# Preparing the look-ups and corner weights of far samples eight rounds at once, ahead of their gathers

## The reference, cut to what matters

```python
loc_x = px + kx + off[..., 0];  loc_y = py + ky + off[..., 1]
x0 = floor(loc_x);  y0 = floor(loc_y);  wx = loc_x - x0;  wy = loc_y - y0
sampled = corner(y0, x0, (1-wy)*(1-wx)) + corner(y0, x0+1, (1-wy)*wx) \
        + corner(y0+1, x0, wy*(1-wx)) + corner(y0+1, x0+1, wy*wx)   # corners outside the image give 0
out = einsum('nhwkgc,nhwkg->nhwgc', sampled, mask) @ output_proj_w.T + output_proj_b
```

## Time and profile before

| | |
|---|---|
| median of 3 runs | 3149.86 us (3148.06 to 3168.16) |
| the profiled execution | 3152.57 us, span 3150.9 us |
| busy: PE, DVE, ACT, POOL | 86%, 85%, 57%, 40% of the span |
| value stage, first image | about 1597 to 1666 us |
| group stage, first image | about 1670 to 2346 us |
| value stage, second image | about 2407 to 2475 us |
| group stage, second image | about 2480 to 3144 us |
| far lists, rounds in them | 16, 52 in all: 3 3 3 3 5 3 2 4 and 3 3 3 4 3 4 3 3 |

### The profile page before, as it was taken

How to read it: one execution, slowest core, us unless ns; L and a number is a source line. 1 busy time by engine, 2 the same in 40 slices (tenths; PEclk the granted TensorE clock), 3 DMA queues, 4 the chain that set the end, 5 groups by cost and what they waited for, 6 DMA issues and landing times.

```text
span 3150.9 us, 78127 instructions
## 1 busy us (share of the span) xinstructions
PE 2720.6 (86%) x22424; PEld 2186.8 (69%) x22424; DVE 2677.2 (85%) x6553; ACT 1781.7 (57%) x3476; POOL 1273.8 (40%) x1837
## 2 busy tenths in 40 slices
PE   1888888999999999999676999989987879999999
PEld 0555555556555655656566888988876778889888
DVE  3788888888888888888666999989987779999998
ACT  0788888888888888888342333433212333344331
POOL 3333332323333333332435444653560554554541
PEclk9999999999999999999888999999999899999999
DMA  7898897889888888889664445444444544444443
GB/s 183 150 166 159 163 163 134 138 142 144 138 144 136 143 139 141 140 141 143 192 202 123 130 144 151 138 136 141 122 148 144 173 125 127 140 129 125 136 114 109
DMA packets 429629, 453.44 MB, mean 144 GB/s; under 512 B 80781, under 2 KB 346397, under 8 KB 428420
## 3 DMA queue, kind: packets, MB, share of 16 engines
q1 hardware_dynamic: 414276, 442.74, 63.7%
q0 software_dynamic: 15168, 8.36, 2.2%
HBM read 294.58 MB, written 156.62 MB: 143 GB/s over the span
## 4 chain that ended last, share of the span: by engine, by line
DVE 25%; issue 9%; DMA 7%; PE 5%; POOL 3%; DVEq 1%; POOLq 1%; ACT 1%; SPq 0%; ACTq 0%
DVE prod L1731 18%; DMA vring<-vals 3%; DVE tt L1715 2%; PE sum_ps L1529 1%; DMA vring<-attended 1%; DMA o_sel<-off_out,pos 1%; DVE my L1710 1%; DVE x L1742 1%; POOL gath L1311 1%; PE wt_ps L1459 1%; DVE x L1646 1%; PE om_ps L1444 1%; PE sum_ps L1481 1%; PE sum_ps L1430 1%; DVE reach L1667 1%
## 5 line engine op out<-in xcount | busy, mean ns | idle before, releaser
L753 ACT ACTIVATE prob<-sbias,nmax 128x256 f32<-128x256 f32 x2048 | 904.0, 501 | 203.0 <-DVE nmax L846 200.6
L846 DVE CUSTOM_DVE_ANT_0 sbias<-s_ps,nbias 128x256 f32<-128x256 f32 x2048 | 768.0, 420 | 212.3 <-PE s_ps L638 201.4
L1731 DVE TENSOR_TENSOR prod<-vring,wt_ps 128x1920 f32<-128x1920 f32 (+3 forms) x512 | 900.9, 1812 | 14.1 <-DMA vring<-vals 12.0
L1481 PE MATMUL sum_ps<-ident,prod 128*128 128x128 f32 x6400 | 751.2, 275 | 24.9 <-DVE prod L1731 24.5
L651 PE MATMUL pt_ps<-ident,prob 128*128 128x128 f32 x4096 | 644.3, 280 | 141.1 <-ACT prob L753 138.0
L1481 PEld LDWEIGHTS sum_ps<-ident,prod 128*128 128x128 f32 x6400 | 719.4, 142 | 66.3 <-DVE prod L1731 42.3
L651 PEld LDWEIGHTS pt_ps<-ident,prob 128*128 128x128 f32 x4096 | 447.3, 140 | 285.1 <-DVE probT L855 133.4
L1583 ACT ACTIVATE hat<-off,one_col 128x576 f32<-128x576 f32 x128 | 140.2, 1095 | 619.3 <-DVE tt L1715 619.3
L571 POOL CAST parts<-qk 128x1024 bf16<-128x1024 f32 x64 | 66.3, 1036 | 869.5 <-ACT qk L746 869.5
L638 PE MATMUL s_ps<-stack 96*128 96x256 bf16 x2048 | 396.1, 274 | 9.0 <-DMA stack<-parts_dram 7.8
L855 DVE COPY probT<-pt_ps 128x512 f32<-128x512 f32 x512 | 351.8, 687 | 12.0 <-PE pt_ps L651 12.0
(11 more groups left out here) (183 smaller groups left out, 3444.4 us busy)
## 6 DMA issues: line engine op xcount, KB each, us to landing
stack<-parts_dram SPq DMA_DIRECT2D x768, 128.0 KB, 7.6
vring<-vals SPq DMA_DIRECT2D x270, 320.0 KB, 3.0
parts_dram<-parts SPq DMA_DIRECT2D x64, 768.0 KB, 6.6
off_out<-off SPq DMA_DIRECT2D x64, 432.0 KB, 4.0
strips<-x SPq DMA_DIRECT2D x68, 256.0 KB, 3.7
far_sums<-nothing SPq DMA_DIRECT2D x64, 256.0 KB, 2.1
attended<-on SPq DMA_DIRECT2D x256, 64.0 KB
x<-x SPq DMA_DIRECT2D x64, 256.0 KB, 4.7
```

Of the source, the lines that this page charges most:

```text
L753: ins = nc.scalar.activation(prob[:, n % 4, half, :], sbias[:, n % SBIAS, half, :], ACT.Exp, bias=nmax[:, n % SBIAS, half:half + 1], scale ...
L846: ins = nc.vector.tensor_tensor_reduce(out=sbias[:, n % SBIAS, half, :], in0=s_ps[:, n % 2, half, :], in1=nbias[:, h, half, :], scale=1.0, ...
L1481: mm = nc.tensor.matmul(sum_ps[:, par, r * H:(r + 1) * H], prod[:, r % 2, dx, dy * C:(dy + 1) * C], ident[:], start=(r + dx + dy == 0), st ...
L1731: nc.vector.tensor_tensor(prod[:, r % 2, first:last].rearrange("p a (t c) -> p (a t) c", c=CG), vring[:, at:at + wide].rearrange("p a (t c ...
```

## The change

- **Rounds at once.** `prepare(e, slot)` issues the look-ups of all 8 possible rounds of an epoch (16 indirect DMAs, two semaphores in turn, so that pair t waits for pair t - 2), then `corner_weights` computes place, index and weights of all 8 rounds with wide small instructions. It waits only for `flags` and for the offsets in DRAM, not for the count of rounds. `far_list` then runs the rounds, each only with a copy of its index, two gathers, three arithmetic steps and the scatter. The gathers of round t + 1 are issued inside round t.
- **Order on POOL.** In each image `prepare` of epoch 0 stands before the wait for the stored `vals`; `prepare` of epoch e + 1 stands behind list e.
- **No mf.** `find_far` no longer computes `mf`; `tap_terms` reads the mask straight from `off`, every third number. The hat functions of a far sample are zero on all but the corners that fall on near taps, and the near taps keep these; `corner_weights` sets the same corners to zero in the far part (`edge`, `held`).
- **Value stage.** From v = 12 ACT normalises every step; POOL is done with v = 11. `flags` of epoch 0 moves from behind v = 7 to behind v = 10. PE makes both halves of group 0's weights after v = 24, and DVE's `tap_terms` of group 1 stands between the value stage and group 0 instead of inside group 0.

```diff
-                for v in (*range(1, V_LAST, 2), *range(V_LAST, GROUPS)):
+                for v in range(1, V_FIRST, 2):
                     normalise(v)
-                for slot in range(VROWS):
-                    pool.wait_ge(vrow_out[slot], count((b + 1) * (4 * GROUPS)))
...
+                def corner_weights(n, flagged):
+                    step(nc.gpsimd.tensor_tensor(wm[:, 0:n], o_sel[:, 0:n, 2], flagged, ALU.mult))
+                    step(nc.gpsimd.tensor_scalar(sidx[:, 0:n], i_sel[:, 0:n, 3], sum_e[:, 0:1], None, ALU.add))
...
+                    then(nc.gpsimd.tensor_tensor(w4[:, 0:n], w4[:, 0:n], held[:, 0:n], ALU.mult))
+
+                def gather_corners(index):
+                    then(nc.gpsimd.tensor_copy(idx1[:], index))
                     for dx in range(2):
-                        gather(gath[:, dx, :], table, idx[:], gathered, dx * YP * C)
...
+                        gather(gath[:, dx, :], table, idx1[:], gathered, dx * YP * C)
+                def far_round(weights, place, look_ahead):
                     pool.wait_ge(gathered, 32)
                     clear(gathered)
...
+                    look_ahead()
                     then(nc.gpsimd.tensor_tensor(gsum[:, 0], gsum[:, 0], gsum[:, 1], ALU.add))
+                    pool.wait_ge(scattered, 16)
+                    clear(scattered)
+                    step(nc.gpsimd.tensor_copy(sidx1[:], place))
                     then(nc.gpsimd.tensor_tensor(gval[:], gsum[:, 0, 0], gsum[:, 0, 1], ALU.add))
...
+                def prepare(e, slot):
+                    n = b * EPOCHS + e
+                    pool.wait_ge(key_ready, count(5 * n + 5))
+                    pool.wait_ge(off_stored, count(16 * (b * GROUPS + EPOCH * (e + 1) + RING_O)))
+                    epoch_base(e)
+                    for t in range(ROUNDS):
+                        if t >= 2:
+                            pool.wait_ge(fetched[t % 2], 32 * (t // 2))
+                        look_up(t, far_at[:, slot, 0, t:t + 1], far_at[:, slot, 1, t:t + 1])
+                    for par in range(2):
+                        pool.wait_ge(fetched[par], 32 * (ROUNDS // 2))
+                        clear(fetched[par])
+                    corner_weights(ROUNDS, far[:, slot, 0:ROUNDS])
...
+                prepare(0, 0)
+                for slot in range(VROWS):
+                    pool.wait_ge(vrow_out[slot], count((b + 1) * (4 * GROUPS)))
+                with pool.Fori(0, EPOCHS // RING_E - 1) as i:
                     for slot in range(RING_E):
+                        far_list(RING_E * i + slot, slot)
+                        prepare(RING_E * i + slot + 1, (slot + 1) % RING_E)
+                far_list(EPOCHS - RING_E, 0)
+                prepare(EPOCHS - 1, 1)
+                far_list(EPOCHS - 1, 1)
...
-                    nc.vector.scalar_tensor_tensor(out=mf[:, s.place], in0=reach[:], scalar=1.0,
-                                                   in1=off[:, s.place, :, :, 2],
-                                                   op0=ALU.is_le, op1=ALU.mult).then_inc(det_step, 1)
...
-                    nc.vector.tensor_tensor(my[:], hat[:, :, :, KG:], mf[:, s.place].unsqueeze(1)
+                    nc.vector.tensor_tensor(my[:], hat[:, :, :, KG:], off[:, s.place, :, :, 2].unsqueeze(1)
...
-                        if v == 2 * EPOCH - 1:
+                        if v == V_FIRST - 2:
                             flags(first_spot(EPOCH - 1))
...
                 each_step(dve, value)
+                tap_terms(first_spot(1))
                 each_group(dve, group)
```

More of the change, by code:

```diff
@@ L1044, in deformable @@
         gathered = ctx.enter_context(nc.semaphore("gathered"))
-        fetched = ctx.enter_context(nc.semaphore("fetched"))
+        fetched = [ctx.enter_context(nc.semaphore(f"fetched{par}")) for par in range(2)]
         scattered = ctx.enter_context(nc.semaphore("scattered"))
         off_stored = sem("off_stored")
+        no_index = sem("no_index")
         block = ctx.enter_context(nc.Block())
@@ L1319, in clear, with look_up @@
                     pool.sem_clear(s)
-                def look_up():
-                    gather(i_sel[:], info_out, pos[:, 0:1], fetched)
-                    gather(o_sel[:], off_now[0], pos[:, 1:2], fetched)
+                def look_up(t, info_at, off_at):
+                    gather(i_sel[:, t, :], info_out, info_at, fetched[t % 2])
+                    gather(o_sel[:, t, :], off_now[0], off_at, fetched[t % 2])
                 def epoch_base(e):
@@ new lines, in far_rest @@
+                                step(nc.gpsimd.tensor_copy(rest_at[:, 0:1], rest_atf[:]))
+                                then(nc.gpsimd.tensor_scalar(rest_at[:, 1:2], rest_atf[:], row_at[:, 0:1], None, ALU.add))
+                                look_up(0, rest_at[:, 0:1], rest_at[:, 1:2])
+                                pool.wait_ge(fetched[0], 32)
+                                clear(fetched[0])
+                                corner_weights(1, is_far[:])
+                                gather_corners(idx[:, 0:1])
@@ L1504, in group @@
                     par = s.place % 2
-                    weights(s.q, 1)
+                    if not isinstance(s.q, int) or s.q > 0:
+                        weights(s.q, 1)
                     taps(s.q, par, 0)
@@ L1537, in value @@
                         if v == V_LAST:
-                            weights(0, 0)
+                            for half in range(HALVES):
+                                weights(0, half)
                 each_step(pe, value)
@@ L1754, in group @@
                     products(s.q, par, 1)
-                    if s.has(1):
+                    if s.has(1) and (not isinstance(s.q, int) or s.q > 0):
                         tap_terms(s.on(1))
```

170 lines of the change are left out of this document (89 added, 81 removed).

## The result

| | before | changed |
|---|---|---|
| median | 3157.82 us (3148.06 to 3168.16, 4 runs) | 3239.38 us (3232.99 to 3243.93, 4 runs) |
| profiled execution, its span | 3152.57, 3150.9 | 3236.43, 3234.8 |
| busy: PE, DVE, ACT, POOL | 86%, 85%, 57%, 40% | 85%, 83%, 56%, 40% |

The change is slower: ratio 1.0247, 95% interval 1.022 to 1.0274, some 80 us. My range ended at 3137. The runs are compared as ratios to runs of the kernel before on the same chip, whose median lay between 3151 and 3164.

What follows compares the result with a forecast made beforehand. Three of 16 far lists, the first of each image and the fifth of the first, were taken to bound the kernel through their length. 32 + 7 + 3.4 = 42.4 us off 3152.57 gave 3110, as median 3108; range 3082 to 3137.

Steps and rivals of the forecast that it cites:

- the length of prepare: On POOL, look-ups and corner weights of all 8 rounds: 36 us, 41 for epoch 0; bounds 31 to 61.
- the later lists: POOL's prepare plus list, 67 us for 3 rounds or 74 for 4, fits the epoch of some 82 us: no cost.
- the epoch of 81.9 us: Sign in the changed profile: 81.9 us between two MAX8 of DVE, 82.7 before less mf.
- a new round: In POOL's list, scatter to scatter: 7.6 us where it took 13.14.
- both first lists in time: First list of each image ready about when PE asks for fsum: 16 us saved each, 32 in all; bounds 8 to 18 each.
- fifth list: List of 5 rounds in the first image done before it is needed: 7 us saved, bounds 0 to 7.
- mf and `my` together: On DVE, mf dropped saves 0.47 us a group, my's strided mask read adds 0.32: 3.4 us less in all.
- value stage: Value stage and group 0: DVE's course 1.4 us earlier in each image; bounds 3 later to 4 earlier.
- the first (lists stay late): Prepare of epoch 0 ends late, PE still waits 12 to 15 us at first lists: 3138 us, chance 0.19.
- the second (a stride that costs nothing): DVE's my reads the mask with its stride at no cost: 19 us more gained, 3089 us, chance 0.14.
- The third: POOL becomes the bound from a prepare of 52 us, every list late: near 3200 to about 3270 us, chance 0.09.
- The fourth: prepare(0) waits for something stored late and starts 5 us later; inside the forecast's range, no chance of its own.

Runs made afterwards that it cites:

- four rounds ahead: The changed kernel with rounds 0 to 3 looked up in prepare, rounds 4 to 7 inside the list only where it has more than 4 rounds: 3122.84 us, ratio 0.9879.
- late prepare: Prepare of epoch 0 put behind the wait for the stored vals: 3147.75 us against four rounds ahead as base, 3286.42 us on the changed kernel.
- four rounds alone: The changed kernel with look-ups for rounds 0 to 3 only, the fifth round of one list left out of the output: 3120.39 us, ratio 0.9875.
- paced run: The changed kernel with each pair of look-ups waiting for the pair just before it, not the one two back: 3171.18 us, ratio 1.004.
- burst on the old kernel: The kernel before with 16 more indirect look-ups, read by nobody, behind every list: 3275.71 us, ratio 1.0369.
- the one with indices of round 0: The changed kernel with all eight pairs of look-ups taking the indices of round 0: 3259.47 us, ratio 1.0315.
- six rounds ahead: The kernel with four rounds ahead, now with six, so 12 look-ups in a prepare: 3175.64 us, ratio 1.004.
- the break in the burst: The changed kernel with POOL waiting before the fifth pair of look-ups until the first eight have landed: 3184.94 us, ratio 1.0076.
- 32 partitions: The kernel before with 16 unread look-ups behind every list, each for 32 partitions instead of 128: 3332.45 us, ratio 1.055.

## Why the prediction was wrong, step by step

**The step that failed** is the one on the length of prepare, with its line on the later lists ("It fits. Nothing."): it put the price of the look-ups for PE at nothing and gave no reason. I asked of 16 indirect DMAs what POOL needs for them and whether they land in time, and both answers were right: `prepare(2)` took 30.4 us (1791.30 to 1821.68), `prepare(0)` 33.2 (1630.48 to 1663.63), where I had 36 and 41. I never asked what they do to the engine that sets the time. Before, no more than two look-ups went out in a row, with gathers and small steps around them; that those rows showed no harm said nothing of sixteen. The price, from changed kernel to four rounds ahead, is 3239.4 - 3122.8 = 117 us by the medians and 108 between the two profiled executions. Of the 108, the value stages are 12.1 and 7.4 (first product 82.0 and 82.2 us after the first `vring`, with four ahead 69.9 and 74.8), and what follows the first product of each image is 37.9 and 52.4; against that the changed kernel's first `vring` came 1.9 earlier. A steady epoch loses 89.4 - 82.2 = 7.2; the epoch with the list of five rounds loses 3.2, since with four ahead that list costs 4.7 again, and the last burst of the first image costs some 2.

Of the signs that I had named, `fsum`, `size`, `my` and the scatters came as forecast; the epoch of 81.9 us did not, and it is the one that stands for the whole path.

| step | predicted | measured |
|---|---|---|
| a new round | 7.6 us | 7.6 in the mean, 6.7 to 9.2 (36 rounds of the changed kernel, scatter to scatter) |
| both first lists in time | 32 us | 25 to 30 (four ahead against late prepare) |
| fifth list | 7 us | 7.9 with four rounds alone (90.1 to 82.2 an epoch), 3.2 where its fifth is looked up in the list; 0.5 of either is mf's |
| `my` | 1.37 us | 1.35 |
| mf and `my` together | 3.4 us less | 0.11% less, -0.1% to 0.32%; 0.5 us an epoch |
| value stage | 2.8 us less | 0.14% less, -0.08% to 0.36% |
| burst of look-ups | not in the sum | 117 us more by the medians, 108 in the traces |

The sum without the last row was 42 us; four rounds ahead brings some 38 (0.9879 x 3149.86 = 3112). So 3108 was near what the kernel takes when its look-ups come in eights; the change doesn't make them so.

**Of the rivals**, the first (lists stay late) and the second (a stride that costs nothing) did not come: the stride costs what the earlier trace rows said. The Trainium skill ("SBUF — State Buffer", Door 1: The DMA port swizzle) says that accesses which cross to a new 16-byte line pay a penalty, and the trace agrees (`my` 1.35 us, before 1.05). The third ended on the right side by the wrong mechanism. It had POOL become the bound and `fsum` late; in the changed kernel PE never waits for `fsum`. It came only in the paced run, where prepare grew beyond what an epoch holds. My 0.09 for slower stood on POOL's time alone. The fourth did not come: `prepare(0)` started at 1630.5.

**The first list** started later than I wrote: its first corner gather waited until 1679.67 for the stored `vals`, since the value stage was late; it still ended before PE asked.

## What to carry to other kernels

A batch of indirect DMAs costs more than its issuer's time: eight in a row were harmless in the group stage here, twelve and sixteen stopped PE, and waiting for each pair before the next, which also halved their pace, did away with it. Before batching look-ups, count how many go out without a break, fetch ahead only what is nearly always used (four rounds here, not eight), and leave the rare rest to where it is known to be needed. When an engine pauses for "issue" inside a block whose inputs are all ready, look for what another queue is doing just then, not for a semaphore.

## What the runs showed of the hardware

What the runs show is that 16 indirect look-ups in a row make PE stutter (burst on the old kernel: ratio 1.0369), that 16 in pairs don't (1.004), and that eight in a row don't in the group stage (epochs of 82.2 us). What links them to PE they don't show. One candidate was that PE's instructions arrive late.

The packets of instruction fetches stand in the profile as queues of their own. In the group stage a packet of 16 KB on q8 comes once in some 15 to 16 us, and mostly 100 to 145 matmuls with their weight loads lie between two of them (median 119), so q8 carries PE's. The page of DMAs cut to one burst of the changed kernel (1793 to 1814) has no instruction row; the same view of the paced kernel over its 16 look-ups (1965 to 2002) has both kinds:

```profile
q1 hardware_dynamic: 1356, 1.72, 27.9%
q0 software_dynamic: 507, 0.03, 7.3%
```

```profile
q1 hardware_dynamic: 6497, 6.46, 56.3%
q0 software_dynamic: 448, 0.03, 3.8%
q8 instruction: 3, 0.05, 0.8%
q14 instruction: 2, 0.02, 0.1%
```

Counted from 1 to 21 us after the first look-up, q8 has 14 packets in the 48 bursts of the changed kernel, the one with indices of round 0 and the one with the late prepare, where its usual pace would give 62; in the paced kernel, in 16 such windows, 20 where it would give 21. That looks as if the look-ups held back PE's instructions. Three counts from the same traces speak against it:

- A packet comes when PE has gone through its usual number of instructions, burst or not. In the intervals between packets that hold the start of a group-stage burst of the changed kernel PE ran 107 to 143 matmuls, with four rounds ahead, where it doesn't stop, 121 to 139. With four ahead the packet after a burst's start comes mostly 14 to 18 us after it; PE's own stop moves it to mostly 21 to 26, out of the 20 us that were counted. The missing packets can be the effect of the stop.
- With six rounds ahead PE runs on without a pause from some 17.5 us, in 11 of the 13 group-stage bursts in which it stutters 0.4 to 3.2 us before the packet comes.
- With the break in the burst, PE begins to stutter at 21 us, in 11 bursts 3 to 9 us after a packet came, and so it does in four bursts on the old kernel (2 to 6 us after one).

The Trainium skill ("DMA: Bandwidth & Descriptors", Queues, rings and completion order) says that each DMA engine takes the queues it has work for in turn, packet by packet; by that rule a fetch would not wait for a burst to end, and the DMA engines were far from full (27.9% and 7.3% of their time above). These counts don't contradict it. So the link between look-ups and stutter is open. Also open is why 32 partitions are worse than 128; the pace of 1.17 against 1.25 us is the only difference that I can name.
